# Wider router products and an earlier first weight load in a cross-attention and mixture-of-experts kernel

## The reference

```python
x = x + tanh(g_xattn) * einsum('emk,enk->emn', quant_1x128(layernorm(x)), quant_128x128(ctx))
xr = layernorm(x).reshape(2048, 512)
probs = softmax(xr @ Wg)                          # 8 experts
gate_vals, expert_idx = top_k(probs, 2)           # each expert takes at most 640 tokens
h = relu(einsum('ecd,edf->ecf', dispatched, w1))  # 512 -> 2048
expert_out = einsum('ecf,efd->ecd', h, w2)        # 2048 -> 512
x = x + tanh(g_ffn) * combine(gates, expert_out)
```

## Time and profile before

| | us |
|---|---|
| median of 3 runs | 875.39 |
| lowest, highest | 875.11, 876.22 |
| the profiled execution | 875.59 |
| its span in the trace | 873.7 |
| TensorE busy | 818.2 (94%) |
| TensorE weight loads | 396.1 (45%) |
| VectorE busy | 601.3 (69%) |
| ScalarE busy | 358.2 (41%) |
| GpSimd busy | 222.6 (25%) |

### The profile page before, as it was taken

The page is one execution under the profiler, slowest core; times in us unless marked ns, Lnnn a source line. Parts: engine busy times, 40 slices in busy tenths (PEclk is TensorE's granted clock), DMA queues, the critical chain, the costliest instruction groups (busy, mean ns, idle before and its releaser), DMA issues.

```text
span 873.7 us, 12297 instructions
## 1 busy us (share of the span) xinstructions
PE 818.2 (94%) x4377; PEld 396.1 (45%) x4378; DVE 601.3 (69%) x954; ACT 358.2 (41%) x586; POOL 222.6 (25%) x218
## 2 busy tenths in 40 slices
PE   0588899799999999999999999999999999999996
PEld 0434658444444444444444444444444444444442
DVE  6999987476577786788577667756785678565430
ACT  4888986243314451435142514251435043414310
POOL 3133021666323033204300331033203320232010
PEclk9999986599999999999999999999999999999998
DMA  8604143795377254727462747263726382512000
GB/s 304 276 1 181 69 153 146 218 190 121 85 146 264 103 149 139 268 96 143 150 220 96 144 134 239 96 144 122 251 96 123 119 276 96 112 57 61 1 26 24
DMA packets 79258, 123.18 MB, mean 141 GB/s; under 512 B 43358, under 2 KB 43374, under 8 KB 75136
## 3 DMA queue, kind: packets, MB, share of 16 engines
q1 hardware_dynamic: 68032, 93.33, 34.8%
q0 software_dynamic: 10912, 29.50, 12.1%
q10 hardware_dynamic: 288, 0.00, 0.0%
HBM read 96.52 MB, written 18.95 MB: 132 GB/s over the span
## 4 chain that ended last, share of the span: by engine, by line
PE 82%; DVE 4%; DMA 4%; ACT 3%; issue 2%; SPq 2%; POOL 1%; POOLq 0%; ACTq 0%; DVEq 0%
PE mm L852 37%; PE mm L782 36%; DMA w_stage<-in_L_ffn_w 3%; PE mm L570 2%; PE mm L822 2%; PE mm L761 1%; PE xT_ps L596 1%; PE mm L580 1%; SPq L327 1%; SPq L326 1%; PE mm L596 1%; DVE region L1251 1%; ACT region L909 1%; DMA lists<-notes,goals 1%; DMA region<-x_split,row_next 1%
## 5 line engine op out<-in xcount | busy, mean ns | idle before, releaser
L852 PE MATMUL mm<-region,w_split 128*128 128x512 f16 x1536 | 335.4, 381 | 2.0 <-ACT region L1004 1.5
L782 PE MATMUL mm<-region 128*128 128x512 f16 x1536 | 335.8, 379 | 0.0
L852 PEld LDWEIGHTS mm<-region,w_split 128*128 128x128 f16 x1536 | 150.7, 98 | 185.4 <-issue 5.0
L782 PEld LDWEIGHTS mm<-region 128*128 128x128 f16 x1536 | 148.8, 98 | 181.3 <-issue 4.2
L1125 ACT ACTIVATE region<-mm 128x512 f16<-128x512 f32 x128 | 76.5, 598 | 310.3 <-PE mm L852 310.3
L1571 DVE SCALAR_TENSOR_TENSOR region<-mm,region 128x512 f16<-128x512 f32 x128 | 88.5, 692 | 110.7 <-ACT region L1125 110.7
L496 POOL DMA_INDIRECT out<-region,back_now x40 | 62.0, 1549 | 171.4 <-DVE region L1584 137.3
L1574 DVE SCALAR_TENSOR_TENSOR region<-w_stage,w_scale,region 128x512 f16<-128x512 f32 x128 | 96.2, 752 | 0.0
L1128 ACT ACTIVATE region<-w_stage,w_scale 128x512 f16<-128x512 f32 x128 | 91.4, 714 | 0.0
L1344 DVE TENSOR_REDUCE top<-w_stage 128x1 f32<-128x512 f32 x112 | 76.0, 678 | 2.3 <-DMA w_stage<-in_L_ffn_w 2.3
L1357 DVE SCALAR_TENSOR_TENSOR w_split<-w_stage,w_scale,w_split 128x2048 f16<-128x2048 f32 x32 | 74.0, 2348 | 4.4 <-ACT w_split L888 2.6
(11 more groups left out here) (195 smaller groups left out, 599.9 us busy)
## 6 DMA issues: line engine op xcount, KB each, us to landing
w_stage<-in_L_ffn_w SPq DMA_DIRECT2D x64, 1024.0 KB, 5.4
region<-in_x SPq DMA_DIRECT2D x4, 1024.0 KB, 13.2
x_split<-region SPq DMA_DIRECT2D x8, 512.0 KB, 2.8
out<-region SPq DMA_DIRECT2D x4, 1024.0 KB, 5.3
w_stage<-in_ctx SPq DMA_DIRECT2D x2, 1024.0 KB, 11.7
region<-in_ctx SPq DMA_DIRECT2D x2, 1024.0 KB, 14.9
region<-x_split,row_next POOLq DMA_INDIRECT x40, 5.0
region<-out,row_next POOLq DMA_INDIRECT x40, 4.5
```

The source lines that it names most:

```text
L782: mm = pe.matmul(mm2[s % 2][:, :], hidden[:, hh, f, s * P:(s + 1) * P], w2_split[:, wh, f, :], start=(f == 0 and hh + wh == 0), stop=(f == ...
L852: mm = pe.matmul(products(f), w1_split[:, wh, k, f * P:(f + 1) * P], xT[:, xh * KD + k, 0:WIDE], start=(k == 0 and wh + xh == 0), stop=(k ...
```

## The change

In the router the four products of a tile move `wg_sb[:, k, :]` eight times over (a broadcast with stride zero, `COPIES` = 8): 64 columns, written to columns 8 `i` to 8 `i` + 63 of the same bank. Tile `i`'s own eight columns are the first of them; the rest is overwritten by the tiles that follow, or read by nobody.

In SyncE's queue quarter 0 of expert 1's first weights is issued when the fourth gathered slot has landed, ahead of the fifth slot's wait and transposition. In the loop the load of quarter 0 moves from the head of a body to the end of the one before, so that the order of all other transfers stays; the last body is written out. Each load gets one more semaphore increment (`alone`) ahead of it.

```diff
+COPIES = 8
...
                 if W1_TILES[k] > 0:
                     alone(sp, q["sp_passed"])
                     sp.wait_ge(q["mm1_done"], after * NF + W1_TILES[k])
+                alone(sp, q["sp_passed"])
                 sp.dma_start(w1_stage[:, k, :], w1_t[e, :, k, :]).then_inc(w1_in[k], 16)
...
                 sp.wait_ge(q["w2_lo"], after * NF + WF * (k + 1))
+                alone(sp, q["sp_passed"])
...
+            sp.wait_ge(x_got[FULL - 1], 16)
+            alone(sp, q["sp_passed"])
+            load_w1_part(1, 0, 0)
             sp.wait_ge(x_got[FULL], 16)
             sp.dma_start_transpose(xT[:, :, FULL * P:NS * P], x_slots[:, FULL, :]).then_inc(xT_in[FULL], 16)
-            with nc.sync.Fori(0, E - 1) as e:
-                load_w1_part(e + 1, 0, e)
+            def weights(e):
                 load_w1_part(e + 1, 1, e)
                 load_w1_part(e + 1, 2, e)
                 load_w2_part(e + 1, 0, e)
...
                 turn_slots(e + 1)
+
+            with nc.sync.Fori(0, E - 2) as e:
+                weights(e)
+                load_w1_part(e + 2, 0, e + 1)
+            weights(E - 2)
...
+                    bank = mm1[0][:, 1, :] if g >= 2 else spare_ps
                     for k in range(KD):
-                        mm = pe.matmul(logits_of(g)[:, i, :], xnT[:, m, k, :], wg_sb[:, k, :],
-                                       start=(k == 0), stop=(k == KD - 1))
+                        mm = pe.matmul(bank[:, i * E:(i + COPIES) * E], xnT[:, m, k, :],
+                                       wg_sb[:, k, :].unsqueeze(1).broadcast_to([P, COPIES, E]),
+                                       start=(k == 0), stop=(k == KD - 1), skip_group_check=True)
```

## The result

| | before | after |
|---|---|---|
| median, runs of the comparison | 876.10 (7 runs) | 872.22 (7 runs) |
| lowest, highest | 874.18, 880.89 | 868.69, 873.19 |
| the profiled execution | 875.59 | 872.49 |
| its span | 873.7 | 870.5 |
| mean granted clock of the span | 0.971 | 0.978 |

The ratio is 0.994 with an interval of 0.991 to 0.997: faster by 0.6%, some 5 us. On the 875.4 us that the forecast started from this is 870.1. The forecast of 867.8 (7.8 us) was too far: 870.1 lies within its wide range (866.5 to 871.5), not within the forecast's own (866.6 to 869.2). The seven executions aren't spread evenly: two took 868.7 us, one 870.6, and four 872.2 to 873.2. The profiled one is of the upper group.

What follows compares the result with a forecast made beforehand. TensorE's matmuls were taken to bound the kernel, with time to win only before 177 us, where the clock halves around router batches. 875.6 less 7.3 (clock) less 0.5 (load) gave 867.8 us; own range 866.6 to 869.2, wide 866.5 to 871.5.

Steps and rivals of the forecast that it cites:

- Direct cost 0 ns: Router products on TensorE: moving 64 columns instead of 8 hides under the next weight load, adding 0 ns per instruction.
- The first two stretches: TensorE's half-clock times 106.4 to 113.2 and 120.0 to 123.4 us go to full clock: 2.0 us kept, 3.8 together.
- The walk: Engine-by-engine retiming from 106.4 us to the third choice, each instruction at its own duration and order: 7.3 us gained.
- The third stretch: TensorE's half clock from 137.1 to 149.9 us goes to full; VectorE becomes late, total gain reaching 7.3 us.
- The block behind it: Third choice at 150.13 to first expert product at 166.24 us moves as one block; 1 us either way.
- The slow start of the expert: Expert's first products stay at half clock until 171.2 us before, 4.7 us and more; carried at 1 us either way.
- the note lists: TensorE's later 1.5 us wait, where GpSimd's last five scatters follow the sixteenth hidden tile: moves along and stays.
- The load: Expert 1's first weight quarter goes out 3.8 us earlier; VectorE's wait and TensorE's 0.53 us go: 0.5 us gained.
- Unhidden columns: Rival, router products: columns don't hide behind weight loads, 47 ns each; 1.8 us of gain lost, 869.7 us; chance 0.10.
- Partial clock: Rival, router batches: full clock holds in only some of the slow stretches; 869.5 to 875 us; chance 0.065.

Runs made afterwards that it cites:

- the change's second profile: The unaltered change timed once more, in ten executions, against the kernel before: median 869.31 us, ratio 0.994.
- GpSimd held: The change, with GpSimd's low halves of tiles 10 and 11 waiting until VectorE has written the first choice; against the kernel before: 868.41 us, ratio 0.993.
- the one that gives GpSimd more work: The change with GpSimd held, and VectorE's low halves of the last two tiles given to GpSimd; against the kernel before: 870.57 us, ratio 0.995.
- the gap filled: The change, with four unread f16 products of 512 columns in TensorE's gap ahead of the first places; against the kernel before: 869.50 us, ratio 0.994.
- 8 columns with GpSimd held: The early load and GpSimd held, but the router moves 8 columns as before; against the kernel before: 873.56 us, ratio 0.997.

## Why the prediction was right or wrong

**Direct cost 0 ns: right.** 112 and 213 ns in both kernels; with 128 columns it is 110 to 114 ns at full clock. The rule of the Trainium skill that was weighed against it (TensorE: Matmul & The Clock Gate, Part 3, "What overlaps and what doesn't"), that a weight load overlaps a running product only when their row groups differ, doesn't hold for these f32 products: by it 64 columns would have cost 47 ns more.

**The first two stretches: right.** The clock was 1.00 from 103 to 133. The walk put the last tile of the second batch at 116.3, and it was at 115.96. It carried 3.8 us to the 24 router products; counted from the first router product they moved by 2.8 (31.5 to 28.7), and 0.86 of the missing 1.0 is the wait that is the next point.

**The third stretch: the step that failed.** "I assume it stays at 1.00 from 106.4 to the router's end" held, by the mean clocks, in about three of four executions, not in the profiled one nor in three others of the first seven. The walk took each instruction "at its own duration" and left GpSimd out, and so missed that the write of the first choice comes to lie beside GpSimd's instruction. The gap of 0.86 us is both a small cost of its own and, in some executions, what goes ahead of the fall. Where the clock falls, the third choice is 45.0 us after the first router product instead of 40.5: 1.8 us of the forecast 7.3 are gained.

**The walk where the clock held: 1.0 us too optimistic, all of it GpSimd.** 7.3 us were forecast for the third choice. From the first router product it is 46.8 us before, 40.5 in the change's second profile (6.3 us), 40.0 with GpSimd held (6.8 us). VectorE works without a pause up to the third choice in both, so what its instructions wait for GpSimd counts one for one: 1.1 us in the first (1.29 for 0.20) and 0.6 us with GpSimd held (0.73 for 0.16). That is the whole of the missing 1.0 and 0.5 us. That VectorE becomes late there was right.

**The block behind it: right within its bound, its gain luck.** From the third choice to the first expert product it was 16.1 us and is 16.0 to 16.5 in all runs but the one that gives GpSimd more work (16.9). The slow start of the expert, carried at 1 us either way, lasted 2.8 us here in place of 5.0 (the clock rose at 167.3): 1.1 us, which with the load's 0.5, less the 0.3 more behind the note lists, is nearly the 1.5 us gained after the expert's start. The 1.1 us are a draw and not the change's: in the eleven profiles without products put in ahead of the expert the slow start lasts 2.7 to 6.1 us, and 6.1 and 5.9 are those of two kernels that have the early load as well (the gap filled, and 8 columns with GpSimd held).

**The load: right.** Both waits went. Its price alone came out at 1.4 us, with 0.5 inside the interval. The transfers do crowd each other, as far as one profile of each kernel shows: the fifth slot's transposition takes 13.4 us from issue in place of 6.2 and the gathers of output rows 9.2 in place of 4.1, but nothing waited for them, as the first reader of the transposition starts at 217.8.

**What is left open.** The third stretch doesn't explain all of the 2.8 us that are missing. In the second set nine of ten executions held the clock, and the ratio is 0.994 again, 5.0 us. 1.0 us is GpSimd's wait. The remaining 1.8 us no trace shows: the one execution of that set with a trace is its fastest, 7.6 us under the profiled one of the kernel before (868.00 against 875.59), and has one of the shortest slow starts, 2.7 us. The forecast set one execution's stretches against a kernel whose single executions lie between 872.0 and 880.9 us.

**Slips in the working.** None moves the forecast. The clock row of before has two slices at 6 and 5 between 131 and 175 us, and an 8 ahead of them, not three at 6. Unhidden columns would have given 869.6, not 869.7. The chances of the cases add up to 1.03.

**The rivals.** Partial clock had 0.065 at 869.5 to 875. It describes the profiled execution and the median of the first seven, and was under-weighted, above all because one profile was taken for the kernel before: the 8-column kernel loses more or fewer stretches from one execution to the next, and so does the wide one.

## What to carry to other kernels

A walk that moves work forward must be read again for what then lies side by side on engines that share something; here shifts of 2.6 and 4.1 us made two instructions meet that had followed each other. Where the granted clock takes part, one profile is one draw: compare several executions, and look at each one's mean clock before pricing a stretch. Columns that ride under a weight load cost next to nothing here, and with them the clock held where it had fallen; try them where narrow products stand ahead of dense work.

## What the runs showed of the hardware that wasn't expected

A write of 64 f16 numbers a partition by VectorE took 1.29 us beside a GpSimd instruction and 0.20 us without, and five one-hots 3.44 us against 1.57. One on 3 f32 numbers a partition (`std_b`) took 0.73 us against 0.16. An f32 product instruction with a weight load of its own goes at 112 ns at 2.4 GHz whether it moves 8, 64 or 128 columns, and at 213 ns at 1.2 GHz with 8 or 64. With no change in the program the clock fell at 133 us in one execution and held until 146 us in another, each with the same 0.86 us gap on TensorE.
